# Attention scores: each head in its own 32 partitions of the stacked queries and keys, plain and turned scores issued alternately, other PSUM banks

## The chip, the cores and the metric

The kernel runs on one core of a Trainium2 chip. The metric is the device time of one execution in microseconds (us); lower is better. TensorE multiplies, VectorE (DVE) and ScalarE (ACT) and GpSimd (POOL) work on elements, SyncE (SP) issues the DMAs. PE in a row of the profile is a matmul of TensorE and PEld a load of its stationary operand.

## The reference, cut to what matters

Four residual layers act on `x`, 64 batches of 64 channels by 256 positions. The change touches only the first, a gated cross attention with 8 heads of 8 channels:

```python
x = x + jnp.tanh(g_xattn[0]) * _L0_xattn_ref(_layernorm(x, axis=-1), ctx_2048, ...)
# in _L0_xattn_ref(x, c, ...): b=64, h=8 heads, kc=8 channels of a head, 256 positions
q = _rope(_proj(Wq, bq, x) per head, 4);  k = _rope(_proj(Wk, bk, c) per head, 4);  v = _proj(Wv, bv, c) per head
scores = jnp.einsum('bhqd,bhkd->bhqk', q, k) / jnp.sqrt(kc)
out = jnp.einsum('bhqk,bhkd->bhqd', jax.nn.softmax(scores, axis=-1), v)
return _proj(Wo, bo, out)
```

A mixture of experts, a gated pooling and a feed-forward layer follow. They are the same code in both kernels.

## The kernel before, in words

The attention works on 32 tiles `n` of two batches each (128 channels on the partitions, 256 positions along them), so 16 heads (`HP`) a tile. It is a pipeline over tiles written out by hand: each engine runs the same `body(n, c, i)` for n from -2 to 33, of which the first four and the last four are unrolled and the others run in a loop of four (`steps`). Each body has 16 slots, `s_` 0 to 15, and in body n an engine does its share of the projections of tile n+2, of the plain scores of tile n+1 and of the turned scores of tile n, in the order that the slots give.

A score is computed twice. The plain score (line 510) has queries on the partitions and keys along them: DVE takes its maximum along each row (`tensor_reduce`, line 369) and nothing else is done with it. The turned score (line 527) has keys on the partitions; the row maxima are subtracted in the product itself, by extra rows of the stacked operands, and ACT takes its exponential into `e_t` (line 422). Then `e_t` is multiplied with the values (line 546, "PV" below), 8 products for each group of four heads, each into its own 32 columns of the array and its own 32 partitions of `o_ps`.

Queries and keys are split into a high and a low fp32r part, and three products of parts make one score. These lie as stacked rows: `q_st` holds 96 rows (three times 32: four heads of a unit by 8 channels) and 8 rows for the maxima (`m_rows`); `k_st` has a copy for each of the four heads `j` of a unit, with zeros in the rows of the other three heads. So every score product runs over 96 or 104 rows of the array. A DMA of 32 KB puts each piece of a key there, 12 for a tile (line 211), three of 128 KB the queries (line 225).

PSUM has 8 banks of 2 KB a partition. `s_ps` has two buffers of two banks (a pair of heads each), `st_ps` two of one bank, `o_ps` and `misc` one each. `misc` is used in turn by everything else that TensorE makes: the projections of keys and queries (line 433), the values (471), the turned maxima (461), the turned outputs (488, 494) and the output projection (441). The plain scores of pair g wait for `max_taken` of pair g-2; the turned ones of a head wait for the exponential two heads back.

DVE also makes the statistics of the layer norm (305, 310), normalizes (331), applies the rotation with the bias (295), adds the bias of the values (342) and normalizes the outputs (352, 356). POOL adds the two terms of the rotation (260), splits the sum into high and low (268, 270), makes the reciprocal deviation (247, 249) and adds the result to x (254).

## Time and profile before

| | us |
|---|---|
| median of 3 runs (lowest to highest) | 1603.46 (1603.43 to 1603.86) |
| the profiled execution's own time | 1603.07 |
| its span, first to last instruction | 1601.4 |
| attention, until its last addition to x ends | 588.6 |
| PE busy over the span | 1450.3 |
| DVE, ACT, POOL busy over the span | 957.3, 779.5, 525.7 |

The page divides the span into 40 slices. The attention is the first 14 of them and most of the next. TensorE is busy for 90% or more of the third to the fourteenth slice, and the granted clock is at nine tenths or more of full speed in each of these 14. Matmuls are pipelined, so a busy TensorE says that one is under way, not that the array is full: times between starts tell more than durations. In a timeline, one row stands for consecutive instructions of one line, "x4" says how many, and square brackets hold the idle time of the engine before them and what ended it.

### The profile page before, as it was taken

Reading aid. Unit: us, or ns where it says so; the run is one execution under the profiler, and the core shown is the slowest. Engines: PE = TensorE matmul, PEld = TensorE weight load, DVE = VectorE, ACT = ScalarE, POOL = GpSimd, SP = SyncE. Lnnn points to the kernel's source line nnn. Section 1 sums busy time; section 2 is a strip of 40 time slices with the busy share of each in tenths; the row PEclk is TensorE's granted clock in tenths of the full one; section 3 lists DMA queues with packets and bytes.
Section 4 is the critical chain, followed back from the end, with each engine's and each line's share of the span. In section 5 each row is a group of like instructions: output and inputs, shape, how many; then the busy total and the mean of one; then the engine's idle time right before and its main releaser. Section 6 shows DMA issues by size and latency. Waiting matters only on the chain. (4 is left out here: it accounts for less than half of the span.)

```text
span 1601.4 us, 32051 instructions
## 1 busy us (share of the span) xinstructions
PE 1450.3 (91%) x10096; PEld 1207.3 (75%) x10097; DVE 957.3 (60%) x1819; ACT 779.5 (49%) x1427; POOL 525.7 (33%) x586
## 2 busy tenths in 40 slices
PE   4899999999999958999898999999916599999998
PEld 3677777777777737888787888888805478888887
DVE  6888887878888726766664333333323366666643
ACT  3466666666666653332233333333313366666652
POOL 4332332323323113644356333200041355555220
PEclk9999999999999987999999999999955599999999
DMA  5122122121121112211373323211170001111000
GB/s 170 57 58 63 50 62 55 52 61 53 53 62 52 45 33 67 92 54 53 122 235 109 92 92 92 66 52 52 44 244 0 27 27 40 40 41 40 15 14 27
DMA packets 89017, 106.54 MB, mean 67 GB/s; under 512 B 12144, under 2 KB 80368, under 8 KB 88304
## 3 DMA queue, kind: packets, MB, share of 16 engines
q1 hardware_dynamic: 79488, 75.69, 15.8%
q0 software_dynamic: 9456, 29.89, 5.8%
q8 instruction: 43, 0.70, 0.2%
q14 instruction: 30, 0.25, 0.0%
HBM read 54.29 MB, written 25.03 MB: 50 GB/s over the span
## 5 line engine op out<-in xcount | busy, mean ns | idle before, releaser
L422 ACT ACTIVATE e_t<-st_ps 128x512 f32<-128x512 f32 x512 | 277.9, 595 | 165.4 <-PE st_ps L527 164.9
L369 DVE TENSOR_REDUCE row_max<-s_ps 128x4 f32<-128x1024 f32 x256 | 311.0, 1217 | 34.0 <-PE s_ps L510 33.8
L510 PE MATMUL s_ps<-k_st,q_st 96*128 96x256 f32 x1024 | 197.2, 316 | 14.3 <-DMA q_st<-q_part 13.0
L527 PE MATMUL st_ps<-q_st,k_st 104*128 104x256 f32 x1024 | 170.4, 287 | 1.6 <-ACT e_t L422 1.5
L510 PEld LDWEIGHTS s_ps<-k_st,q_st 96*128 96x128 f32 x1024 | 147.9, 194 | 23.2 <-DMA q_st<-q_part 13.7
L527 PEld LDWEIGHTS st_ps<-q_st,k_st 104*128 104x128 f32 x1024 | 143.9, 190 | 6.6 <-ACT e_t L422 5.2
L546 PE MATMUL o_ps<-e_t,v_st 128*32 128x256 f32 x2048 | 137.1, 385 | 0.9 <-ACT e_t L422 0.9
L1576 POOL DMA_INDIRECT gathered_tail<-sorted_results,result_at x64 | 72.9, 1139 | 153.5 <-POOLq L2046 135.2
L1434 PE MATMUL y_ps_moe<-w_all_moe,h_hi_moe 128*128 x568 | 112.5, 281 | 2.6 <-DVE h_lo_moe L1253 2.6
L1810 DVE TENSOR_TENSOR h_all_tail<-silu_tail,u_ps_tail 128x512 f32<-128x512 f32 x64 | 43.8, 685 | 117.4 <-ACT silu_tail L1684 65.9
L1259 DVE TENSOR_TENSOR h_all_moe<-silu_moe,u_ps_moe 128x512 f32<-128x512 f32 x71 | 48.8, 687 | 106.2 <-PE u_ps_moe L1412 106.2
L1412 PE MATMUL g_ps_moe<-w_all_moe,xt_hi_moe 128*128 x284 | 106.2, 415 | 0.0
L949 ACT COPY y_sb_moe<-y_ps_moe 128x256 f32<-128x256 f32 x71 | 26.5, 373 | 159.3 <-PE y_ps_moe L1434 159.3
L1412 PE MATMUL u_ps_moe<-w_all_moe,xt_hi_moe 128*128 x284 | 99.8, 392 | 0.0
L1434 PEld LDWEIGHTS y_ps_moe<-w_all_moe,h_hi_moe 128*128 128x128 f32 x568 | 92.4, 190 | 6.2 <-issue 3.5
L1249 DVE TENSOR_TENSOR xt_lo_moe<-t_ps_moe,xt_hi_moe 128x256 fp32r<-128x256 f32 x71 | 30.1, 424 | 92.2 <-ACT xt_hi_moe L936 92.2
L818 POOL DMA_INDIRECT sorted_rows<-xn_moe,slots_moe x64 | 64.2, 1004 | 63.1 <-DVE slots_moe L1052 45.8
L546 PEld LDWEIGHTS o_ps<-e_t,v_st 128*32 128x32 f32 x2048 | 53.4, 109 | 40.2 <-ACT e_t L422 1.1
L247 POOL TENSOR_SCALAR var_eps<-mean_var 128x1 f32<-128x1 f32 x32 | 7.5, 235 | 229.8 <-DVE mean_var L310 228.7
L1434 PE MATMUL y_ps_moe<-w_all_moe,h_lo_moe 128*128 x284 | 79.7, 281 | 0.0
L1684 ACT ACTIVATE silu_tail<-g_ps_tail 128x512 f32<-128x512 f32 x64 | 38.0, 594 | 83.9 <-PE g_ps_tail L1964 83.7
L1976 PE MATMUL y_ps_tail<-w_hi_tail,h_hi_tail 128*128 128x256 f32 x256 | 74.1, 289 | 0.5 <-DVE h_lo_tail L1817 0.5
(309 smaller groups left out, 3583.2 us busy)
## 6 DMA issues: line engine op xcount, KB each, us to landing
k_st<-k_part SPq DMA_DIRECT2D x384, 32.0 KB
q_st<-q_part SPq DMA_DIRECT2D x96, 128.0 KB, 3.2
stage_moe<-in_experts POOLq DMA_DIRECT2D x21, 512.0 KB, 4.2
rows_in_moe<-sorted_rows SPq DMA_DIRECT2D x71, 128.0 KB, 2.0
sorted_results<-y_sb_moe SPq DMA_DIRECT2D x71, 128.0 KB
c_in<-in_ctx SPq DMA_DIRECT2D x33, 128.0 KB, 2.1
xn_moe<-in_ctx SPq DMA_DIRECT2D x8, 512.0 KB
context_tail<-in_ctx SPq DMA_DIRECT2D x4, 1024.0 KB, 15.3
```

The costliest lines, as they stand in the source:

```text
L369: nc.vector.tensor_reduce(out, s_ps[s_ // 2 % 2][:].rearrange("p (j h) t -> p j h t", j=2), AX_X, ALU.max).then_inc(s["max_taken"], 1)
L422: nc.scalar.activation(e_t[h % 8][:], st_ps[h % 2][:], ACT.Exp, scale=float(DH) ** -0.5)\
L510: last = nc.tensor.matmul(s_ps[s_ // 2 % 2][:, 2 * (h - s_) + half_, :], q_st[r][0:ROWS, u, half_ * P:(half_ + 1) * P], k_st[r][0:ROWS, u, ...
L527: last = nc.tensor.matmul(st_ps[h % 2][:, half_, :], k_st[r][0:MROWS, u, j, half_ * P:(half_ + 1) * P], q_st[r][0:MROWS, u, :], start=True ...
L546: last = nc.tensor.matmul(o_ps[32 * j:32 * j + 32, u % 2, :], v_st[r][:, half_, u * UH + j, :], e_t[(u * UH + j) % 8][:, half_, :], start= ...
L818: pool.indirect_dma_start(out=xs[:, :], out_offset=bass.IndirectOffsetOnAxis(ap=slots[:, w, GT * j + t:GT * j + t + 1], axis=0), in_=xn[j ...
L1259: nc.vector.tensor_tensor(h_all[c % 2][:], silu[c % 2][:], u_ps[c % 2][:], ALU.mult)\
L1412: last = nc.tensor.matmul(bank[c % 2][:], t[b][:, kc * P:(kc + 1) * P], w_flat[:, bass.ds(where + ((w * 3 + kc) * PIECE + base), FF)], sta ...
L1434: last = nc.tensor.matmul(y_ps[:, 2 * ((c - 1) % 2), :], h[:, m * P:(m + 1) * P], w_flat[:, bass.ds(where + ((w * 3 + 2) * PIECE + m * D), ...
L1576: pool.indirect_dma_start(out=gathered[r][:], out_offset=None, in_=ys[:, :], in_offset=bass.IndirectOffsetOnAxis(ap=result_at[:, q // GT, ...
L1810: nc.vector.tensor_tensor(h_all[m % 2][:], silu[m % 2][:], u_ps[n % 2][:], ALU.mult)\
L1976: last = nc.tensor.matmul(y_ps[:, t, :], h[:, m, t * P:(t + 1) * P], w[:, 2, m * D:(m + 1) * D], start=(m == 0 and b == 0 and t % 2 == 0), ...
```

## The change

The stacked rows are laid out anew. Head j of a unit has partitions 32j to 32j+31 of `q_st` and of `k_st`: three rows for each channel (the three products of parts) and, in every fourth row, the two rows of the maxima (`MAX_ROWS`, 8 rows in all). A score product takes its operands from these 32 partitions alone, so it runs in 32 rows of the array. `k_st` has no copies for four heads any more; 3 DMAs of 128 KB fill it. The rows of the maxima are set to zero in `q_st` by another DMA (`zero_rows`) before the plain scores, and the maxima are written there before the turned ones.

TensorE issues the two products of a turned score and the two of a plain one alternately, one head of each in a slot; they lie in different 32 partitions. The turned scores run 10 slots behind (`LAG`) instead of 8. `s_ps` is now one tensor of three banks; pair p takes two of them in turn (`pair_banks`), and its second head waits for the maxima of the pair just before. `misc` becomes `misc_a` and `misc_b`.

Work moves: the normalization of x from DVE to POOL, in two steps; the bias of the rotation is made once (`turned_bias`) and added on POOL for each tile, so that DVE's rotation is one multiplication of 512 columns; the values are copied by ACT, and their bias goes into `out_bias` once. A pair in banks 0 and 2 needs two reductions on DVE. In the first bodies other buffers are cleared, and eight bodies at the end are unrolled instead of four.

In a body of the changed kernel, TensorE has other work ahead of the scores in slots 1 (turn `a_sb`), 2 (turn the maxima), 3 (project k), 5 (output projection), 6 (project q), 8 (turn `o_sb`), 10 (values) and 14 (turn `o_sb`); PV follows the scores of slots 3, 7, 11 and 15. POOL makes the parts of k, the addition to x, the parts of q and then the normalization of tile n+3. The diff below holds, in this order, the constants, the buffers, SP's stacking, POOL's sum with the bias, DVE's order and its reductions, ACT's copy of the values, and TensorE's scores.

```diff
-    LAG = 8
-    ROWS, MROWS = 96, 104
-    PEEL_FIRST, PEEL_LAST = (-2, -1, 0, 1), (30, 31, 32, 33)
+    PAIRS = HP // 2
+    LAG = 10
+    MAX_ROWS = slice(3, P, 16)
+    PEEL_FIRST, PEEL_LAST = (-2, -1, 0, 1), tuple(range(26, 34))
...
-        s_ps = [ps(f"s_ps{r}", [P, 4, D]) for r in range(2)]
+        s_ps = ps("s_ps", [P, 3, 2, D])
...
+        pair_banks = [((0, 1), (0, 2), (1, 2))[p % 3] for p in range(PAIRS)]
+        pair_order = [(1, 0) if p == 0 or p % 3 == 1 else (0, 1) for p in range(PAIRS)]
...
                     sp.wait_ge(s["k_high"], n + 3)
+                    for t in range(2):
+                        sp.dma_start(k_st[r][t:P:4, :, :].bitcast(F32), part["k"][:, 0, :].bitcast(F32))\
+                            .then_inc(k_stacked[r], 16)
                     sp.wait_ge(s["k_split"], n + 3)
+                    sp.dma_start(k_st[r][2:P:4, :, :].bitcast(F32), part["k"][:, 1, :].bitcast(F32))\
+                        .then_inc(k_stacked[r], 16)
+                    sp.wait_ge(s["q_high"], n + 3)
+                    for t in (0, 2):
+                        sp.dma_start(q_st[r][t:P:4, :, :].bitcast(F32), part["q"][:, 0, :].bitcast(F32))\
+                            .then_inc(q_stacked[r], 16)
...
+                nc.gpsimd.tensor_tensor(bare[a][:], roped[a][:, 0, :], roped[a][:, 1, :], ALU.add)\
+                    .then_inc(s[a + "_summed"], 1)
+                pool.wait_ge(s[a + "_summed"], n + 3)
+                nc.gpsimd.tensor_tensor(whole[a][:], bare[a][:], turned_bias[a][:], ALU.add).then_inc(s[a + "_whole"], 1)
...
+                for p in range(PAIRS):
+                    if p == 0 and there(n, c, 0):
+                        split_max(n, c)
+                    if there(n, c, 1):
+                        take_max(n, c, p)
+                    if p == 1 and there(n, c, 2):
+                        rope_parts("k", n, c)
+                    if p == 3 and there(n, c, 2):
+                        rope_parts("q", n, c)
+                    if p == 4 and there(n, c, -1):
+                        normalize_out(n, 0)
+                    if p == 5 and there(n, c, 3):
+                        stats_of(n, 3)
+                    if p == 7 and there(n, c, -1):
+                        normalize_out(n, 1)
...
+                if high == low + 1:
+                    last = nc.vector.tensor_reduce(out, s_ps[:, low:high + 1, :, :], AX_X, ALU.max)
+                else:
+                    for at, bank in enumerate((low, high)):
+                        last = nc.vector.tensor_reduce(out[:, at, :], s_ps[:, bank, :, :], AX_X, ALU.max)
...
+                        nc.scalar.copy(v_st[r][:, :, :, 0:DH],
+                                       misc_a[:, 0:2 * P].rearrange("p (a h d) -> p a h d", a=2, d=DH))\
+                            .then_inc(s["v_stored"], 1)
...
+                rows = slice(32 * j, 32 * j + 32)
+                return [(s_ps[:, pair_banks[p][at], half_, :], q_st[r][rows, u, half_ * P:(half_ + 1) * P],
+                         k_st[r][rows, u, :]) for half_ in range(2)]
...
+                        wait_count(pe, s["exp_done"], HP * (n + k) + h - 1)
+                        wait_alone(pe)
...
+                        wait_count(pe, s["max_taken"], (n + 1) * PAIRS + s_ // 2 - (s_ + 1) % 2)
+                    for half_ in range(2):
+                        if turned:
+                            out, w, of = turned[half_]
+                            last = nc.tensor.matmul(out, w, of, start=True, stop=True)
+                            if half_ == 1:
+                                last.then_inc(s["st_scored"], 1)
+                        if scores:
+                            out, w, of = scores[half_]
+                            last = nc.tensor.matmul(out, w, of, start=True, stop=True)
+                            if half_ == 1 and s_ % 2 == 1:
+                                last.then_inc(s["scored"], 1)
```

## Rows read from the trace of the kernel before

**Rows 1.** Busy time by stretch: us, PE, PEld, DVE, ACT, POOL, granted clock, DMA share, GB/s.
```profile
300.00:400.00 100.00, 99.21 (x901) 78.71 (x902) 80.80 (x138) 63.38 (x124) 30.34 (x53) 1.00 0.21 57
...
590.00:600.00 10.00, 0.95 (x5) 0.96 (x6) 4.96 (x21) 3.12 (x5) 2.22 (x6) 0.50 0.38 127
```
**Rows 2.** Timeline of TensorE, the turned maxima of bodies 1 and 29.
```profile
61.03 0.27 PE L461 MATMUL misc<-ident,m_parts 128*64 128x128 f32 x1
...
534.24 0.27 PE L461 MATMUL misc<-ident,m_parts 128*64 128x128 f32 x1
```
**Rows 3.** Waits, 100 to 500 us: us in total, times, longest us.
```profile
ACT e_t L422 <- PE st_ps L527: 123.0, 165, 1.9
```
**Rows 4.** Groups of instructions, 100 to 500 us: busy us, mean ns of one, idle before.
```profile
L369 DVE TENSOR_REDUCE row_max<-s_ps 128x4 f32<-128x1024 f32 x190 | 231.2, 1217 | 21.7 <-PE s_ps L510 21.5 <-issue 0.2
...
L510 PE MATMUL s_ps<-k_st,q_st 96*128 96x256 f32 x760 | 144.8, 313 | 0.0
...
L546 PE MATMUL o_ps<-e_t,v_st 128*32 128x256 f32 x1520 | 101.7, 385 | 0.0
...
L342 DVE TENSOR_TENSOR v_st<-misc,bias_v 128x128 f32<-128x128 f32 x48 | 11.5, 281 | 0.0
```
**Rows 5.** Timeline of TensorE over one body: start us, us from first start to last end.
```profile
249.98 0.82 PE L510 MATMUL s_ps<-k_st,q_st 96*128 96x256 f32 x4
...
252.90 1.07 PE L546 MATMUL o_ps<-e_t,v_st 128*32 128x256 f32 x16
253.90 0.66 PE L488 MATMUL misc<-ident,o_sb 128*128 128x128 f32 x4
254.31 0.72 PE L510 MATMUL s_ps<-k_st,q_st 96*128 96x256 f32 x4
254.87 0.64 PE L527 MATMUL st_ps<-q_st,k_st 104*128 104x256 f32 x4
255.35 0.61 PE L488 MATMUL misc<-ident,o_sb 128*128 128x128 f32 x4
...
258.08 0.72 PE L510 MATMUL s_ps<-k_st,q_st 96*128 96x256 f32 x4
...
261.65 1.13 PE L433 MATMUL misc<-c_in,w_in 128*128 128x256 f32 x4
262.43 0.82 PE L510 MATMUL s_ps<-k_st,q_st 96*128 96x256 f32 x4
...
266.88 0.83 PE L510 MATMUL s_ps<-k_st,q_st 96*128 96x256 f32 x4
```
**Rows 6.** Timeline of DVE in the same body.
```profile
254.59 0.26 DVE L352 RECIPROCAL o_rcp<-misc 128x16 f32<-128x16 f32 x1 [0.69 <-PE misc L488]
...
255.09 1.22 DVE L369 TENSOR_REDUCE row_max<-s_ps 128x4 f32<-128x1024 f32 x1
...
258.84 1.23 DVE L369 TENSOR_REDUCE row_max<-s_ps 128x4 f32<-128x1024 f32 x1 [0.91 <-PE s_ps L510]
259.98 0.42 DVE L305 BATCH_NORM_STATS2 stats<-x_sb 128x6 f32 x1
...
260.71 0.18 DVE L316 TENSOR_SCALAR m_parts<-row_max 128x32 fp32r<-128x32 f32 x1
...
261.10 1.23 DVE L369 TENSOR_REDUCE row_max<-s_ps 128x4 f32<-128x1024 f32 x1
```
**Rows 7.** Timeline of the first bodies, where a plain score waits for a maximum.
```profile
35.99 4.62 DVE L369 TENSOR_REDUCE row_max<-s_ps 128x4 f32<-128x1024 f32 x4
...
37.27 0.74 PE L510 MATMUL s_ps<-k_st,q_st 96*128 96x256 f32 x4 [0.84 <-DVE row_max L369]
```
**Rows 8.** Timeline of POOL in the same body as rows 5.
```profile
251.32 0.73 POOL L260 TENSOR_TENSOR q_whole<-q_roped 128x256 f32<-128x256 f32 x1 [2.35 <-DVE q_roped L295]
...
252.69 0.73 POOL L270 TENSOR_TENSOR q_part<-q_whole,q_part 128x256 fp32r<-128x256 f32 x1
```
**Rows 9.** DMA issues of the page: KB each, median us from issue to landing.
```profile
q_st<-q_part SPq DMA_DIRECT2D x96, 128.0 KB, 3.2
```

More of the change, by code:

```diff
@@ L273, in _ @@
+                    row = x_row(n - 2)
+                    nc.gpsimd.tensor_tensor(row, row, like_row(n, y_sb), ALU.add).then_inc(s["y_free"], 1)
+                if there(n, c, 2):
+                    parts_of("q", n, c, i)
+                if there(n, c, 3):
+                    normalize(n, 3)
             steps(pool, body)
@@ L286, in _, with rope_parts @@
+            dve.wait_ge(s["bias_summed"], 2)
             clear_values((0,))
[L287 to L291 removed]
+            def rope_parts(a, n, c):
                 dve.wait_ge(s[a + "_projected"], n + 3)
                 wait_count(dve, s[a + "_summed"], n + 2)
[L294 to L298 removed]
@@ new lines, in take_max @@
+            def take_max(n, c, p):
+                g = (n + 1) * PAIRS + p
+                dve.wait_ge(s["scored"], g + 1)
+                if p == 0:
+                    wait_count(dve, s["m_split"], n)
+                u, j = 2 * p // UH, 2 * p % UH
+                out = row_max[(c + 1) % 2][:].rearrange("p (j u h) -> p j u h", j=UH, u=UNITS)[:, j:j + 2, u, :]
+                low, high = pair_banks[p]
+                if high == low + 1:
[3 more added lines that the diff above has]
+                        last = nc.vector.tensor_reduce(out[:, at, :], s_ps[:, bank, :, :], AX_X, ALU.max)
+                last.then_inc(s["max_taken"], 1)
@@ L437, in body, with score_turned @@
+            def score_turned(c, k, h):
+                r, u, j = (c + k) % RING, h // UH, h % UH
+                rows = slice(32 * j, 32 * j + 32)
+                return [(st_ps[h % 2][:, half_, :], k_st[r][rows, u, half_ * P:(half_ + 1) * P], q_st[r][rows, u, :])
+                        for half_ in range(2)]
             def body(n, c, i):
                 for s_ in range(HP):
-                    if s_ == 0 and there(n, c, -2):
-                        pe.wait_ge(s["a_taken"], n - 1)
-                        nc.tensor.matmul(misc[:, 0:D], w_out[:], a_t[:], start=True, stop=True)\
-                            .then_inc(s["y_projected"], 1)
@@ L445, in body @@
+                    if s_ == 3 and there(n, c, 2):
                         if isinstance(n, int) and n < 2:
@@ L530, in body @@
-                        last.then_inc(s["st_scored"], 1)
+                                pe.wait_ge(ones_in, 16 * RING)
+                        wait_count(pe, s["exp_done"], HP * (n + k) + h - 1)
+                        wait_alone(pe)
+                    if there(n, c, 1):
+                        scores = score(n, c, s_)
+                        if s_ == 0:
+                            pe.wait_ge(q_stacked[(c + 1) % RING], 64 * uses(c, i, 1))
+                            pe.wait_ge(k_stacked[(c + 1) % RING], 48 * uses(c, i, 1))
+                            if isinstance(n, int) and n == -1:
+                                pe.wait_ge(ones_in, 16 * RING)
+                        wait_count(pe, s["max_taken"], (n + 1) * PAIRS + s_ // 2 - (s_ + 1) % 2)
@@ L550, in body, with turn_out, value_bias @@
                         last.then_inc(s["pv_done"], 1)
-            steps(pe, body)
+            def turn_out(b):
+                for half_, u in ((h, u) for h in range(2) for u in range(2)):
+                    at = (2 * half_ + u) * P
+                    last = nc.tensor.transpose(misc_b[:, at:at + P], o_sb[b][:, u, half_ * P:(half_ + 1) * P],
+                                               ident[:])
+                last.then_inc(s["o_turned"], 1)
+            def value_bias():
+                pe.wait_ge(more_consts_in, 3 * 16)
+                nc.tensor.matmul(misc_b[:, 0:1], w_out[:], bias[:, 5:6], start=True, stop=True)\
+                    .then_inc(s["value_bias_made"], 1)
+            steps(pe, body, None, value_bias)
 def experts(nc, dram, x, ident, tanh_gain, xs, ys, result_at, shares, attn, half_rotated):
```

419 lines of the change are left out of this document (183 added, 236 removed).

## The prediction

> **What bounds the kernel now.** I read the busy time by stretch first, to find the stage. In the attention TensorE is busy 99.2 of 100 us, DVE 80.8, ACT 63.4, POOL 30.3, at the full clock [rows 1]. The maxima of bodies 1 and 29 are turned 473.2 us apart, 28 bodies of 16.90 us each [rows 2]; these 28 are what the change can move. Then the waits: ACT waits for turned scores 123 us in 400, TensorE for nobody to speak of [rows 3]. So a body lasts as long as TensorE's instructions take, and the starts in its timeline say which. Between the first and the last of rows 5 lie 31 rows, one body. A group of four score products in mid-stream takes 0.48 us, 0.12 each (254.87 to 255.35), up to 0.66 where another kind of work has come before it; the 16 groups make 9.5 us. The four PVs take 1.00 each, start to next start [rows 5], 4.0 in all. The rest (projections, turns) adds to 3.35. Sum 16.9.
>
> PV shows what the change is after. One of its products lasts 385 ns on average, yet 16 are through in 1.00 us [rows 4, 5], because four neighbours use different columns and run together. The scores, 313 ns each on average [rows 4], run one behind the other.
>
> **TensorE after the change.** The same 64 score products, each over 32 rows, in 16 slots of two turned and two plain. No row of before shows products in different rows of the array at once. Bounds for a slot: nothing overlaps, 4 x 0.12 = 0.48; the two kinds overlap fully, 0.24. I take 0.24, nearest to PV's rows, where four overlap. 16 x 0.24 = 3.84, in place of 9.5. The Trainium skill (TensorE: Matmul & The Clock Gate, Part 3, "Measured speedup vs the span model") gives 3.07 times for four such row groups, 77% of the full factor; 77% of two would make a slot 0.31. No run here has shown it yet; by it the sum would be 16 x 0.07 = 1.1 us a body dearer on TensorE, part of it before pairs that DVE waits for.
>
> What it adds on TensorE: changes between products of 32 rows and full ones. The price is read at PV, which is of another shape than its neighbours: four passes of a full fp32 product take 0.78 (261.65 to 262.43), so four rounds of PV should take 0.78 and take 1.00 [rows 5]; 0.22 for entering and leaving, 0.11 a change. Eight groups of other work now stand between scores, one of them right behind a PV: 15 new changes, 1.65 us. They cost nothing at the least (turns and scores now follow each other without loss, 0.41 + 0.56 for eight products [rows 5]), and I put the upper bound at 0.3 each, nearly the whole of a product in flight. The skill speaks against the change here (TensorEngine Tiling (Array Packing), Key Properties): changing the tiling mode drains TensorE. It has no price; by rows it is the 0.11. TensorE: 3.84 + 4.0 + 3.35 + 1.65 = 12.8 us a body, 4.1 under now.
>
> **DVE after.** Its starts price it: a reduction of 1024 holds it for 1.14 (258.84 to 259.98); statistics 0.73 (to 260.71), split of the maxima 0.39 (to 261.10), normalizing half the outputs 0.50 (254.59 to 255.09) [rows 6]. From 281 ns for 128 columns and 1217 for 1024 [rows 4] a column costs 1.045 ns; so 512 columns take 0.68, or 0.59 in a row of them, and the new rotation 0.6. Five reductions of 1024 and three pairs of 512: 5 x 1.14 + 3 x 1.18 = 9.2; rotations 1.2, outputs 1.0, statistics 0.73, split 0.39: 12.5 us. Now it is 13.7 (80.8% of 16.90). Gone are the normalization of x and the bias of the values.
>
> **The wait that is added.** This decides the size. Before, a pair of plain scores needed the maxima of two pairs back, and DVE was never in the way. With three banks, the second head of pair p (slot 2p+1) waits for the maxima of pair p-1, and since that wait stands ahead of the slot's turned products too, everything on TensorE queues behind it. DVE in turn cannot begin pair p until that slot is done. The round trip: from DVE's end to TensorE's start 0.06 (first of four reductions ends at 37.21, product at 37.27 [rows 7]); first to last product of the slot 0.13, and 0.08 that a first product takes longer; from the last product's start to DVE 0.32 (group at 258.08, last product 0.44 later, reduction at 258.84 [rows 5, 6]). With the 0.08 by which a reduction's end lies behind its hold, DVE stands idle for 0.67 to 0.69 between two maxima unless it has something else to do. Its other work covers that after pair 5 (statistics) and between tiles (outputs and split), and nearly after pairs 1 and 4; after pairs 2 and 6, and after pair 0, there is none.
>
> Walked through a body, zero where the last maxima of the tile before are known, pairs at TensorE's slots: pair 0 is scored at 0.5, DVE comes at 0.8 (outputs, split), done 1.9. Pair 1: TensorE waits for the split, turns, projects k, scored 2.8; DVE idle 0.8. Two reductions, rotation, 4.5. Pair 2 follows PV and the output projection, 4.7, idle 0.2, done 5.8. Pair 3 waits for it behind the projection of q: 6.5, idle 0.7; maxima and rotation to 8.3. Pair 4 after PV and turn: 8.5, idle 0.2; to 10.2 with the outputs. Pair 5: 10.3, idle 0.2; to 12.2 with statistics. Pair 6 in time; to 13.3. Pair 7: 14.0, idle 0.7; to 15.2, known 15.3. So 12.5 of work and 2.8 of idle time: 15.3 us.
>
> **POOL and the queue.** One more sum of 0.73 for k and for q each, and two or so for x [rows 8]: 5.1 to 8.1 us, hidden by itself. But the chain to the next tile's plain scores gets longer. q is rotated at 8.3; POOL is just through with k and x, and needs 2.1 (251.32 to 253.42 [rows 8]) and 0.89 for the extra sum: 11.5. The last of three DMAs leaves SP at about 11.9 and lands 3.2 later [rows 9], at 15.1. Slot 0 would start at 14.7 (15.3 less the 0.57 to its pair's end). It comes 0.4 late; DVE, busy until 16.1 with outputs and split, and the 0.8 of idle time at pair 1 absorb nearly all. I add 0.1: 15.4 us. The 9 DMAs a body instead of 17 don't shorten it.
>
> ACT gets one copy (about 0.3) to its 10.7: 11.0, hidden while it is the third engine. If it weren't, that would be 0.3 a body.
>
> **Sum.** 28 bodies x 1.5 = 42 us. At the start TensorE waits for the queue chain, which grows by the extra sums: 2 us dearer over bodies -1 and 0; what is cleared there differs little. At the end the bodies without projections gain about 1 each, two more slots of lag cost one: -3 in all. 1603.1 (the profiled execution, 0.4 under the median) - 42 + 2 - 3 = 1560. The other layers stay. With 15.0 to 16.0 a body the forecast's own range is 1543 to 1577.
>
> **The rivals.** *The hand-over hardly binds* (0.16): DVE meets its scores in time except at the three places where nothing covers the trip, 12.5 + 3 x 0.69 = 14.6, saves 2.3 a body, 1538. For it: TensorE has 2.6 us to spare. Against: that slack isn't where the waits are.
>
> *Changes between shapes are dear* (0.16): at 0.3 each they add 15 x 0.19 = 2.9 on TensorE, of which about 1 falls before pairs that DVE waits for: 16.4, 28 x 0.5 = 14 saved, 1588. A quarter of this case ends within 0.2% of now.
>
> *Rows don't overlap* (0.13), the change doesn't do what it says: a slot takes 0.48, pairs are scored 0.23 later behind each wait, and TensorE, 16.6 us busy, comes late at pairs 2, 4 and 5. The same walk gives 17.6, and 28 x 0.7 = 20 more: 1623. This is the rival on the other side: the new wait is paid and nothing is had for it. A slot of 0.38 is about where it turns. Against it stands PV in the trace.
>
> *The clock falls* (0.05), as it does where TensorE is idle between stages, 0.50 [rows 1]. What products over a quarter of the rows do to the clock, no row shows. TensorE's 12.8 at half speed is nearly 24 us with waits: 1800. Nothing in the trace points to it; PV, with few columns a product, runs at 1.00.
>
> **How the numbers follow.** The forecast has 0.50. The range takes in the hand-over rival and the dear changes, 1534 to 1605, and leaves out the last two, 0.18. Faster by over 0.2% (below 1600.3, about what a measurement of this kernel tells from no change): 0.50 + 0.16 + 0.12 = 0.78. Within: 0.04 + 0.01 of the third = 0.05. Slower: 0.12 + 0.05 = 0.17.
>
> **What would show it.** Right: turned maxima 15.4 us apart; plain and turned products starting within 0.02 us of each other; four of a slot in about 0.24; DVE's largest wait is for plain scores, 0.5 to 0.8 us at pairs 1, 3 and 7, and TensorE's for `row_max`; its DMA wait small. Wrong: no such waits on DVE (first rival), gaps on PEld of over 0.3 us at each change (second), products 0.12 apart (third), a clock of 0.5. The prediction fails most easily if TensorE's work lies otherwise between the pairs than I walked it, since idle times of 0.2 stand beside others of 0.8, or if the queue is slower with rows four partitions apart, which no row of before shows.

## The result, and the profile after

The changed kernel takes 1678.26 us, median of 4 runs (1676.05 to 1679.46), against 1603.45 for the kernel before on the same chip: a ratio of 1.0465, 95% interval 1.0452 to 1.0479. It was forecast to be faster, at 1560 us with a range up to 1605; sign and range are both wrong. The profiled execution's span is 1677.8 us, 76.4 longer.

Where these 76.4 us are is read from the turned maxima of bodies 1 and 29, as in [rows 2]. Timeline of TensorE after; the middle two stand around one body at the full clock:

```profile
62.34 0.42 PE L501 MATMUL misc_b<-ident,m_parts 128*64 128x128 f32 x1
...
360.29 0.30 PE L501 MATMUL misc_b<-ident,m_parts 128*64 128x128 f32 x1
...
377.68 0.30 PE L501 MATMUL misc_b<-ident,m_parts 128*64 128x128 f32 x1
...
580.26 0.30 PE L501 MATMUL misc_b<-ident,m_parts 128*64 128x128 f32 x1
```

The 28 bodies last 517.9 us, 18.50 each in place of 16.90: 44.7 of the 76.4. A body in which the clock does not fall takes 17.39, as here (377.68 - 360.29), to 17.5, most often 17.45. From the maxima of body 29 to the end of the attention 82.5 us pass in place of 54.4: another 28.2. The start costs 1.3 and the other layers 2.2. The busy time by stretch, columns as in [rows 1]: the 28 bodies, the tail behind them, the moments before and after one fall of the clock, and 400 us in the middle:

```profile
62.34:580.26 517.92, 469.45 (x4287) 272.41 (x4283) 360.98 (x588) 307.72 (x615) 219.56 (x363) 0.93 0.17 53
580.26:662.80 82.54, 68.19 (x479) 36.86 (x477) 25.76 (x44) 40.39 (x79) 8.81 (x13) 0.66 0.04 12
...
387.80:391.20 3.40, 2.51 (x32) 1.31 (x28) 3.10 (x7) 2.44 (x7) 1.91 (x4) 1.00 0.23 77
391.30:394.60 3.30, 3.30 (x28) 1.77 (x28) 1.88 (x4) 1.49 (x3) 1.46 (x4) 0.50 0.29 88
100.00:500.00 400.00, 363.60 (x3321) 210.87 (x3319) 279.26 (x453) 238.33 (x478) 171.10 (x282) 0.92 0.17 53
```

TensorE, busy 99.2% before, is busy 90.9%, and its granted clock, 1.00 before, is 0.92 to 0.93 in the loop and 0.66 in the tail. It falls to 0.50, the 1.2 GHz level, for about 75 us of the loop in 18 spells of a few us and for 56 us of the tail. The first of the 28 bodies belongs to this too: the clock is on record only from 70.4 us on, but up to there TensorE's rows last as long as at the low level (0.42 for the turn at 62.34, 0.30 for the same turn later), and this body takes 19.69. So three things happened: the body at the full clock got 0.55 longer (28 x 0.55 = 15 us), the low clock in the loop cost 28 x 18.50 - 28 x 17.45 = 29, of it 2 in the first body, and in the tail up to 28. The 28 are an estimate: 56 us at half clock do the work of 28 where TensorE is the limit, and 54.5 would be left, the tail of before. But TensorE idles for 14 of the 82.5 us, so it may be less.

The waits, 100 to 500 us (us in total, times, longest), against [rows 3]:

```profile
ACT e_t L454 <- PE st_ps L561: 162.2, 197, 2.1
...
DVE row_max L368 <- PE s_ps L566: 59.9, 65, 2.1
PEld st_ps L561 <- issue: 57.2, 166, 0.7
DVE row_max L365 <- PE s_ps L566: 52.1, 66, 2.6
...
PEld misc_b L592 <- ACT o_sb L432: 19.9, 21, 0.9
PEld st_ps L561 <- DVE row_max L368: 19.5, 36, 0.8
```

DVE waits 112 us for plain scores in 400/18.5 = 21.6 bodies, 5.2 a body, and TensorE waits for DVE's maxima and for a copy of ACT. Each waits for the other. No DMA is among the large waits. Next, TensorE's timeline in the body behind the 17.39 us one. It starts at 377.68, runs at the full clock up to a fall at 391.2, and takes 18.36:

```profile
378.77 1.13 PE L465 MATMUL misc_a<-c_in,w_in 128*128 128x256 f32 x4 [0.37 <-ACT a_t L422]
...
381.26 0.38 PE L561 MATMUL st_ps<-q_st,k_st 32*128 32x256 f32 x1
381.26 0.38 PE L566 MATMUL s_ps<-k_st,q_st 32*128 32x256 f32 x1
381.48 0.28 PE L561 MATMUL st_ps<-q_st,k_st 32*128 32x256 f32 x1
381.49 0.28 PE L566 MATMUL s_ps<-k_st,q_st 32*128 32x256 f32 x1
381.69 0.70 PE L514 MATMUL misc_b<-a_t,w_out 128*128 128x256 f32 x2
...
388.16 0.38 PE L561 MATMUL st_ps<-q_st,k_st 32*128 32x256 f32 x1 [0.20 <-DVE row_max L368]
...
391.25 1.12 PE L592 MATMUL misc_b<-ident,o_sb 128*128 128x128 f32 x4 [0.75 <-ACT o_sb L432]
```

Turned and plain products start within 10 ns of each other, as was hoped. But the second product of the same 32 rows starts 0.22 after the first, not 0.12 as in [rows 5], and the next work 0.43 after the slot's start. Two at a time, at half the rate each: 0.11 a product, the old pace. The weight loads (PEld) of the same four products:

```profile
381.26 0.18 PEld L561 LDWEIGHTS st_ps<-q_st,k_st 32*128 32x128 f32 x1 [0.41 <-issue]
381.26 0.18 PEld L566 LDWEIGHTS s_ps<-k_st,q_st 32*128 32x128 f32 x1
381.37 0.18 PEld L561 LDWEIGHTS st_ps<-q_st,k_st 32*128 32x128 f32 x1
381.37 0.18 PEld L566 LDWEIGHTS s_ps<-k_st,q_st 32*128 32x128 f32 x1
```

The load for the second half starts 0.11 after the first product did, and the second product another 0.11 later. This is no matter of the 32 rows. In the kernel before, the first step of a group of scores behind other work is 0.20 to 0.22 as well (254.31 to 254.51), and the last one before a PV 0.21 (before a turn, 0.12); the steps between them are 0.12, each load starting together with the running product. The same steps stand in the last bodies of changed_filled_wait (below), where six turned products of the same 32 rows follow each other at the full clock:

```profile
604.82 0.74 PE L563 MATMUL st_ps<-q_st,k_st 32*128 32x256 f32 x4
605.40 0.40 PE L567 MATMUL st_ps<-q_st,k_st 32*128 32x256 f32 x2
605.73 0.30 PE L501 MATMUL misc_b<-ident,m_parts 128*64 128x128 f32 x1
```

Their steps are 0.23, four times 0.12, and 0.21 to the turn. So a slot by itself has no step of 0.12 at all: it is one first step and one last step, 0.43, with two groups of rows or with four.

DVE in the same body, against [rows 6]:

```profile
377.81 1.23 DVE L365 TENSOR_REDUCE row_max<-s_ps 128x4 f32<-128x1024 f32 x1 [0.28 <-PE s_ps L566]
380.39 1.29 DVE L368 TENSOR_REDUCE row_max<-s_ps 128x2 f32<-128x512 f32 x2 [1.35 <-PE s_ps L566]
...
382.89 1.22 DVE L365 TENSOR_REDUCE row_max<-s_ps 128x4 f32<-128x1024 f32 x1 [0.61 <-PE s_ps L566]
384.74 1.23 DVE L365 TENSOR_REDUCE row_max<-s_ps 128x4 f32<-128x1024 f32 x1 [0.62 <-PE s_ps L566]
...
386.81 1.29 DVE L368 TENSOR_REDUCE row_max<-s_ps 128x2 f32<-128x512 f32 x2 [0.25 <-PE s_ps L566]
...
393.22 1.29 DVE L368 TENSOR_REDUCE row_max<-s_ps 128x2 f32<-128x512 f32 x2 [1.43 <-PE s_ps L566]
```

Idle for 0.28 + 1.35 + 0.61 + 0.62 + 0.25 + 1.43 = 4.5 us before six of its eight pairs, where 2.8 was forecast. The two large ones follow TensorE's waits for ACT at 378.77 and 391.25; part of the last is the fall of the clock at 391.2.

A slot does not always take 0.43. When the next slot follows without a wait, its products lie in the other two groups of 32 rows and start before the slot is through, so that both share a first and a last step: two slots then pass in 0.44 to 0.79. TensorE's time in bodies without a fall, added up from start to start of its kinds of work, with its idle time apart (mean us a body, of 11 bodies after the change and 22 or 23 elsewhere; two columns are runs of the next section):

| | before | forecast | tiled_two_banks_each | two_banks_with_handover | after |
|---|---|---|---|---|---|
| scores, 16 slots | 9.4 | 3.84 | 4.8 | 5.65 | 6.3 |
| PV | 4.0 | 4.0 | 4.0 | 4.0 | 4.0 |
| other work, with the changes between shapes | 3.35 | 5.0 | 5.3 | 5.2 | 5.2 |
| idle | 0.1 | 2.6 | 1.8 | 2.1 | 1.9 |
| body | 16.9 | 15.4 | 15.9 | 16.96 | 17.45 |

So a slot takes 0.40 on average after the change, and 0.30 where two banks a pair let the slots follow each other.

### The profile page after: what moved, and what is told of

Read it like the earlier page. It is cut to its first block and busy times, and to the rows that moved or that the text cites. A ratio compares the mean times of both kernels' runs of the same rounds, so it can differ in the third digit from the quotient of the medians.

```text
span 1677.8 us, 32160 instructions
## 1 busy us (share of the span) xinstructions
PE 1472.3 (88%) x10098; PEld 1111.3 (66%) x10099; DVE 931.2 (55%) x1763; ACT 773.8 (46%) x1455; POOL 606.8 (36%) x716
## 5 line engine op out<-in xcount | busy, mean ns | idle before, releaser
L454 ACT ACTIVATE e_t<-st_ps 128x512 f32<-128x512 f32 x512 | 300.0, 600 | 261.9 <-PE st_ps L561 261.1
L365 DVE TENSOR_REDUCE row_max<-s_ps 128x4 f32<-128x1024 f32 x160 | 195.9, 1225 | 90.2 <-PE s_ps L566 86.2
L561 PE MATMUL st_ps<-q_st,k_st 32*128 32x256 f32 x1024 | 230.0, 353 | 16.8 <-DVE row_max L368 6.2
L566 PE MATMUL s_ps<-k_st,q_st 32*128 32x256 f32 x1024 | 228.3, 355 | 16.2 <-DMA q_st<-q_part 6.9
L561 PEld LDWEIGHTS st_ps<-q_st,k_st 32*128 32x128 f32 x1024 | 143.1, 203 | 141.9 <-issue 92.9
L368 DVE TENSOR_REDUCE row_max<-s_ps 128x2 f32<-128x512 f32 x192 | 123.7, 686 | 91.8 <-PE s_ps L566 91.8
L583 PE MATMUL o_ps<-e_t,v_st 128*32 128x256 f32 x2048 | 163.0, 444 | 1.2 <-ACT e_t L454 1.2
L566 PEld LDWEIGHTS s_ps<-k_st,q_st 32*128 32x128 f32 x1024 | 141.0, 203 | 21.4 <-DVE row_max L365 8.4
L273 POOL TENSOR_TENSOR k_bare<-k_roped 128x256 f32<-128x256 f32 x32 | 23.3, 727 | 231.7 <-DVE k_roped L343 231.7
L583 PEld LDWEIGHTS o_ps<-e_t,v_st 128*32 128x32 f32 x2048 | 59.0, 121 | 52.1 <-issue 20.9
```

The costliest lines, as they stand in the source:

```text
L365: last = nc.vector.tensor_reduce(out, s_ps[:, low:high + 1, :, :], AX_X, ALU.max)
L368: last = nc.vector.tensor_reduce(out[:, at, :], s_ps[:, bank, :, :], AX_X, ALU.max)
L454: nc.scalar.activation(e_t[h % 8][:], st_ps[h % 2][:], ACT.Exp, scale=float(DH) ** -0.5)\
L561: last = nc.tensor.matmul(out, w, of, start=True, stop=True)
L566: last = nc.tensor.matmul(out, w, of, start=True, stop=True)
L583: last = nc.tensor.matmul(o_ps[32 * j:32 * j + 32, u % 2, :], v_st[r][:, half_, u * UH + j, :], e_t[(u * UH + j) % 8][:, half_, :], start= ...
```

## The experiments

The theory: a slot of 0.43 by itself means that the new rows gain little on TensorE, the three-bank hand-over costs more than that, and the clock takes the rest. The rivals: the new rows themselves are slow, alternation is needed, the waits for ACT or the moved work are the cost. Each ratio is against the kernel before on the same chip. A run without an interval was timed once, beside medians of the kernel before of 1604 to 1611; "full clock" is the usual body without a fall, and "low" the recorded us at half clock in the loop and in the tail.

**tiled_two_banks_each** is the kernel before with the new rows and the alternate issue alone: `LAG` 8, two buffers of two banks, and DVE's, POOL's and ACT's work as before.

```diff
-    ROWS, MROWS = 96, 104
+    MAX_ROWS = slice(3, P, 16)
...
-        k_st = [sb(f"k_st{r}", [P, UNITS, UH, D], F32R) for r in range(RING)]
+        k_st = [sb(f"k_st{r}", [P, UNITS, D], F32R) for r in range(RING)]
...
+                r, h = (c + 1) % RING, s_ ^ 2
+                u, j = h // UH, h % UH
+                rows = slice(32 * j, 32 * j + 32)
+                return [(s_ps[s_ // 2 % 2][:, 2 * (h % 2) + half_, :], q_st[r][rows, u, half_ * P:(half_ + 1) * P],
+                         k_st[r][rows, u, :]) for half_ in range(2)]
```

> The kernel before with the 32-partition layout alone: one turned and one plain head issued alternately in a slot, but two buffers of two banks for the plain scores, one misc bank, and DVE's, ACT's and POOL's work as before (the plain heads of a unit in another order, so that the two heads of a slot lie in different partitions). Theory 1, pace of the products: two products side by side cost 0.22 us and not 0.12, and a change between shapes some 0.28, so TensorE has 6.9 + 4.0 + 3.35 + 8 x 0.28 = 16.5 us a body and the kernel comes out near 1595, within 15. Theory 2, the hand-over over three banks made the change slow: it is gone here, TensorE's 12.8 us lie under DVE's 13.7, 1510 to 1530. Theory 3, the clock falls because of products over 32 rows: bodies differ by 2 to 4 us among each other as in the changed kernel, 1610 to 1650.

Measured: 1587.84 us (1583.94 to 1590.79), ratio 0.9894 (0.9861 to 0.9928). Most bodies take 15.88 us, and the clock stays at 1.00 in the loop; in the tail it is 0.73:

```profile
100.00:500.00 400.00, 354.43 (x3851) 211.72 (x3843) 345.94 (x579) 270.73 (x529) 130.93 (x227) 1.00 0.20 63
511.60:574.70 63.10, 53.88 (x443) 29.56 (x443) 24.18 (x40) 36.31 (x71) 6.51 (x10) 0.73 0.05 15
```

So the new rows are worth 1.02 us a body, no more, and they alone bring the kernel 1% under the old time: the loop gains 24 us in all, and the tail, with its clock, gives 9 back. That is in the range of the first theory, but not by its sum: the scores take less (4.8) and TensorE stands idle for 1.8 us a body. Two slots that follow each other pass in 0.72 here, not 0.86, and most of the idle time stands before products into the one `misc` bank:

```profile
301.11 0.37 PE L527 MATMUL st_ps<-q_st,k_st 32*128 32x256 f32 x1 [0.25 <-issue]
...
301.40 0.35 PE L527 MATMUL st_ps<-q_st,k_st 32*128 32x256 f32 x1
...
301.83 1.07 PE L549 MATMUL o_ps<-e_t,v_st 128*32 128x256 f32 x16
...
PE misc L468 <- DVE k_roped L295: 15.5, 25, 0.6
...
PE misc L478 <- DVE q_roped L295: 13.7, 26, 0.5
```

**tiled_four_groups** is that kernel with the eight products of two turned and two plain heads together in every second slot, so that all four groups of rows have work at once. The two turned heads then also wait for the exponentials of the two before them together.

```diff
-                    if s_ % 1 == 0:
+                    if s_ % 2 == 0:
                         k, h = st_head(s_)
-                        heads = range(1)
+                        heads = range(2)
```

> As the run before, but in every second slot two turned and two plain heads are issued together: first halves of all four, then second halves, in four different groups of 32 rows. Theory 1: eight products take about 0.44 us instead of 0.88, as in the few places of the changed kernel where two slots met; TensorE 3.5 + 4.0 + 3.35 + 2.2 = 13.1 us a body, under DVE's 13.7 with some waits, 14.3: 1520 to 1540. Theory 2 (hand-over only): the same as the run before, since that is bound by DVE already. Theory 3 (clock): some bodies 2 us and more longer, 1560 to 1600.

Measured: 1601.44 us (1597.99 to 1609.56), ratio 0.9987 (0.9969 to 1.0006): no gain, and outside all three ranges. TensorE's timeline and stretch, then the wait that shows why:

```profile
301.09 0.38 PE L527 MATMUL st_ps<-q_st,k_st 32*128 32x256 f32 x1 [0.38 <-DVE row_max L370]
...
301.32 0.28 PE L532 MATMUL s_ps<-k_st,q_st 32*128 32x256 f32 x1
301.53 0.85 PE L549 MATMUL o_ps<-e_t,v_st 128*32 128x256 f32 x12
...
100.00:500.00 400.00, 321.98 (x3737) 181.04 (x3738) 337.25 (x562) 260.09 (x511) 126.15 (x218) 1.00 0.19 61
...
PEld st_ps L527 <- DVE row_max L370: 57.3, 110, 1.3
```

Eight products pass in 0.44, 0.055 each, no longer than the four of a slot: the factor of two that I had put into a slot is had only by putting more products between the same first and last step. TensorE's busy time falls to 80%, and it waits for DVE instead; the body is 16.4, and the clock stays at 1.00 in the loop.

**two_banks_with_handover** is tiled_two_banks_each, in which the second head of a pair also waits for the maxima just before, as three banks force it to.

```diff
-                            wait_count(pe, s["max_taken"], (n + 1) * (HP // 2) + s_ // 2 - 1)
+                            wait_count(pe, s["max_taken"], (n + 1) * (HP // 2) + s_ // 2 - (s_ + 1) % 2)
```

> The run with the new rows and two banks for each pair of plain scores (body 15.88 us), with one edit: the second head of a pair waits for the maxima of the pair just before, as three banks force it in the changed kernel. The wait isn't needed here; it is put in to read its price alone. If the hand-over between TensorE and DVE is the larger part of the changed kernel's loss: 1 to 1.6 us a body more, 16.9 to 17.5, 1615 to 1635. If that loss comes from the order of work around misc, the two reductions of a split pair and the waits for ACT: under 0.4 us a body, 1586 to 1600. The clock theory (it falls where only products over 32 rows and idle time come together) expects some dips again if bodies get longer.

Measured: 1626.33 us, ratio 1.0128 (1.0106 to 1.0150). The body goes from 15.88 to 16.96 with nothing else touched. The wait alone costs 1.08 us a body, which uses up the gain of 1.02. By the table, 0.84 of it is time in the scores, because neighbouring slots no longer run into each other, and 0.27 is idle time. The rest of the 1.3% lies outside the usual body: 6 us before the loop, 5 in it (mostly its first body and a fall of the clock; low 10), and 10 in the tail.

**changed_half_max** is the changed kernel with the row maximum taken over half of the keys, which halves DVE's share of the round trip.

```diff
-                    last = nc.vector.tensor_reduce(out, s_ps[:, low:high + 1, :, :], AX_X, ALU.max)
+                    last = nc.vector.tensor_reduce(out, s_ps[:, low:high + 1, :, 0:P], AX_X, ALU.max)
```

> The changed kernel, but the row maximum is taken over half of the keys (128 of 256 columns of each head's row), so a reduction holds DVE about half as long; a shift of the exponent cancels in the softmax. DVE's work falls from 12.5 to about 8.4 us a body and each round trip of a bank by 0.5 us. If the hand-over over three banks is what makes the body 17.4 us at full clock: 3 to 4 us a body less, 1560 to 1590. If TensorE's own pace and its waits for ACT do: at most 1 us a body less, 1645 to 1675. The clock theory expects dips as before or more of them, since TensorE has no more to do.

Measured: 1616.4 us, between the two ranges. Full clock 16.65, 0.8 less (22 us); that is what was expected if TensorE's own pace and its waits for ACT set the body, not the 3 to 4 of the hand-over. Low is 10 and 28 in place of 75 and 56. Of the 62 us, 23 more are the low clock in the loop, 13 the tail and 4 the start.

**changed_old_rows** is the changed kernel with the old rows of 96 and 104, and 15 DMAs to stack them; banks, order, `LAG` and moved work stay changed.

```diff
-    MAX_ROWS = slice(3, P, 16)
+    ROWS, MROWS = 96, 104
...
+                    for j in range(2, UH):
+                        for t, of in enumerate((0, 0, 1)):
+                            stack_k(j, t, of)
```

> The changed kernel with the layout alone put back: scores over 96 and 104 rows, 12 pieces of k and one q stack as before; three banks, order, LAG 10 and the work moved to POOL and ACT stay. If the three banks and the order of work are what costs (the two-bank run with the new rows was faster than before), this is no faster than the changed kernel: a slot takes 0.48 instead of 0.43 us and the changes between shapes fall away, 17 to 18 us a body, 1610 to 1670. If the clock falls because of the products over 32 rows, the dips are gone here and all bodies last the same, near 17.4. If it falls because of the idle times of this order, the dips stay.

Measured: 1718.11 us, ratio 1.0671 (1.0638 to 1.0705): worse than the change, outside what I expected of either theory. The body at the full clock is 19.6; low is 11 and 0 in place of 75 and 56, though TensorE is no busier (358.5 of 400 us) and idles 2.1 us a body. The new rows save 2.1 of it. The rest of the change costs 2.7 a body with the old rows (1.9 of it idle time of TensorE), part of it a DMA wait that the new rows do not have:

```profile
PEld st_ps L558 <- DMA k_st<-k_part: 22.2, 21, 1.3
```

**changed_not_alternated** issues the two turned products first, then the two plain ones.

```diff
-                    for half_ in range(2):
-                        if turned:
...
+                    for half_, (out, w, of) in enumerate(turned):
+                        last = nc.tensor.matmul(out, w, of, start=True, stop=True)
...
+                    for half_, (out, w, of) in enumerate(scores):
+                        last = nc.tensor.matmul(out, w, of, start=True, stop=True)
```

> The changed kernel with the two products of the turned score first and then the two of the plain one, instead of alternately. Theory 1: the products of one 32-row group wait for each other's weights (0.22 apart), so only the second turned and the first plain one overlap: about 0.66 instead of 0.43 a slot, up to 3.5 us a body where nothing else waits; 1710 to 1760. If the alternation is worth nothing, because the array takes weights for one product at a time: within 1% of 1678.

Measured: 1681.49 us, as the change. Full clock 17.4 to 17.6, low 68 and 62. A first plain product still starts before the second turned one, which stands ahead of it in the program:

```profile
396.82 0.38 PE L559 MATMUL st_ps<-q_st,k_st 32*128 32x256 f32 x1
396.82 0.38 PE L563 MATMUL s_ps<-k_st,q_st 32*128 32x256 f32 x1
397.04 0.27 PE L559 MATMUL st_ps<-q_st,k_st 32*128 32x256 f32 x1
397.05 0.27 PE L563 MATMUL s_ps<-k_st,q_st 32*128 32x256 f32 x1
```

**changed_copy_earlier** takes the second copy of `o_ps` on ACT a slot earlier, for the wait at 391.25.

```diff
-                    if s_ in (5, 13) and there(n, c, -1):
-                        b = s_ // 13
+                    if s_ in (5, 12) and there(n, c, -1):
+                        b = s_ // 12
```

> The changed kernel with one edit on ACT: the second copy of o_ps stands one slot earlier (12 instead of 13). TensorE's wait in slot 14 for this copy (0.75 to 1.0 us a body, and DVE's 1.4 us before pair 7) shrinks by the 0.5 us of the exponential that goes ahead of it now. If that wait is on the path: 0.4 to 0.6 us a body less, 1655 to 1667, and fewer dips of the clock if the dips come from idle time. If only the bank hand-over binds: within 3 us of 1678.

Measured: 1666.33 us. At the full clock only 0.08 a body is gained: TensorE idles 0.4 less, and its scores take 0.3 more. Low in the loop is 34 in place of 75. The time is in the expected range for the wrong reason.

**new_rows_lighter_dve** adds to tiled_two_banks_each the changed kernel's moves: normalization of x on POOL, copy of the values on ACT, their bias folded.

```diff
-                        nc.vector.tensor_scalar(out, row, mean_var[:, 0:1], rstd[:], ALU.subtract, ALU.mult)\
-                            .then_inc(s["xn_ready"], 1)
...
+                        nc.scalar.copy(v_st[r][:, :, :, 0:DH],
+                                       misc[:, 0:2 * P].rearrange("p (a h d) -> p a h d", a=2, d=DH))\
+                            .then_inc(s["v_stored"], 1)
```

> The run with the new rows and two banks for each pair (1588), and DVE relieved in two places as the changed kernel does it: the normalization of x on POOL, the values copied by ACT with their bias folded in once. DVE's work falls from 13.7 to 12.9 us a body. That run's body of 15.88 us has TensorE 14.1 busy and waits on misc and on DVE's maxima. If DVE's order is what holds misc: 0.4 to 0.8 us a body less, 1565 to 1577. If misc itself does (one bank, each user waits for the one before): under 0.2, 1583 to 1590.

Measured: 1591.31 us, ratio 0.9891 (0.9866 to 0.9915), body 15.88 again. DVE is relieved (330.5 of 400 us busy in place of 345.9) and nothing comes of it, as expected if the one `misc` bank holds TensorE up; the time is 1 us over that range.

**changed_filled_wait** asks whether idle time makes the clock fall: two full products ahead of the wait at 391.25, their result overwritten, and in the bodies without plain scores each turned product three times.

```diff
                         pe.wait_ge(s["o_normed"], 2 * (n - 1) + 1)
+                        for _ in range(2):
+                            nc.tensor.matmul(misc_b[:, 0:D], w_out[:], rope[:, 0, :], start=True, stop=True)
...
+                    if turned and not scores:
+                        for _ in range(2):
+                            for out, w, of in turned:
+                                nc.tensor.matmul(out, w, of, start=True, stop=True)
```

> The changed kernel with work for TensorE in its waits: two full products of 256 columns (0.8 us, results overwritten) ahead of the wait for the copy in slot 14, and in the last bodies, where there are no plain scores, each turned product made three times (same result). If the clock falls because TensorE stands idle there: the dips become rare, bodies 17.5 to 17.7, and the last bodies run at full clock: 1625 to 1650, faster with more work. If idle time has nothing to do with it: dips as before and some 0.2 us a body more, 1680 to 1700.

Measured: 1683.7 us. In the loop low falls to 24 and the mean body to 17.87, and no fall begins at the filled wait any more. In the tail nothing is gained, though TensorE is now busy nearly all the time:

```profile
600.00:655.00 55.00, 53.31 (x327) 36.89 (x327) 3.86 (x13) 20.26 (x38) 1.45 (x2) 0.59 0.01 2
```

**changed_taller_fill** keeps the fill of the loop, and in the last four bodies passes the first half of each PV, over 128 rows, two times more instead.

```diff
-                        for half_ in range(2):
+                        again = 2 if isinstance(n, int) and n >= 30 else 0
+                        for half_, stop in ((0, True),) * again + ((0, False), (1, True)):
```

> The changed kernel with the filled wait in slot 14 as before (two full products), and in the last four bodies, instead of tripled turned products, two more passes of the first half of each PV (128 rows of the array, overwritten by the real one, same result; 1.0 us more for each PV). If the clock falls in the last bodies because products over 32 rows count for less, the work over all rows holds it at full: the stretch from the turned maxima of body 29 to the end of the attention takes 65 to 75 us instead of 82.5 (97.5 with tripled turned products), 1650 to 1668 in all. If any work is as good as another or none helps: 90 us and more, 1675 to 1690.

Measured: 1665.45 us. Low in the tail is 10 in place of 68; the tail itself, 77.2, is a little over what was expected:

```profile
572.50:649.70 77.20, 66.82 (x671) 38.16 (x669) 25.74 (x44) 39.93 (x79) 8.81 (x13) 0.93 0.04 13
```

The mean body is 18.21 with the very loop of the run above (17.87): the falls in a loop scatter by that much.

**changed_short_fill** is the control: the same fill in the loop, over 32 rows, and nothing added in the last bodies.

```diff
-                            nc.tensor.matmul(misc_b[:, 0:D], w_out[:], rope[:, 0, :], start=True, stop=True)
+                            nc.tensor.matmul(misc_b[:, 0:D], w_out[0:32, :], rope[0:32, 0, :], start=True, stop=True)
```

> The control for the filled wait: the same two products of 256 columns ahead of the wait in slot 14 of the changed kernel, but over 32 rows of the array instead of 128 (results overwritten); nothing is done in the last bodies. From the turned maxima of body 1 to those of body 29 the changed kernel had 75 us at the lower clock and 18.50 us a body, with products over all rows 24 and 41 us (two runs) and 17.87 and 18.21. If products over 32 rows count for less: 60 us and more at the lower clock, 18.3 to 18.7 a body, 1673 to 1688. If any product in the wait does as well: 20 to 45 us, 17.8 to 18.2, 1657 to 1668.

Measured: 1661.97 us, ratio 1.0348 (1.0272 to 1.0423), low 24 in the loop, none of it beginning at the filled wait, and 47 in the tail. As a filling of that wait, products over 32 rows help as much as full ones, so my theory that rows are what the clock counts fails there.

**two_banks_taller_fill** puts the same repeats of PV into tiled_two_banks_each.

> The best run so far (new rows, two banks for each pair, 1588) with the same two more passes of the first half of each PV in the last four bodies. There its clock was 0.5 for the last 23 us of the attention, and the stretch from the turned maxima of body 29 took 63.2 us, against 54.3 in the kernel before. If work over all rows holds the clock: 56 to 60 us, 3 to 7 us less in all, 1581 to 1585. If not: 4 to 16 us more, 1592 to 1604.

Measured: 1586.58 us, ratio 0.9892 (0.9865 to 0.9918), between the two ranges. The tail's clock is 0.95 in place of 0.73 and the tail 64.9 us in place of 63.1: the extra products cost what the clock gives back.

Of these, tiled_two_banks_each is the version that beats both kernels. The two others at 0.989 can't be told from it and have more in them.

## Why the prediction was wrong

**The step that failed** is the slot: "I take 0.24, nearest to PV's rows, where four overlap". A slot by itself takes 0.43, and the average slot of the change 0.40; the term 16 x 0.24 = 3.84 measured 6.3. The 0.24 is two steps at the pace of a long run, 0.12. That pace holds within 32 rows too (changed_filled_wait), but a slot has two products of each group and so only a first step of 0.22, behind other work, and a last one of 0.21, before other work. The rows of before had both: groups of four took up to 0.66 behind another kind of work, against 0.48 in mid-stream. I had bounds of 0.24 and 0.48, and took the wrong end. The second half of the step is that the added wait parts neighbouring slots, which would otherwise fill all four groups; the prediction had no term for that. In two_banks_with_handover the scores take 5.65 a body, without the wait 4.8. The Trainium skill's figure (TensorE: Matmul & The Clock Gate, Part 3, "Measured speedup vs the span model") is for four row groups; scaling it to two gave me an estimate of 0.31. This case's traces do not agree with it: a slot by itself takes 0.43, and four groups are 2.2 times as fast as the old pace (eight products in 0.44 against four in 0.48). tiled_two_banks_each comes to 0.30 a slot, but because its slots run into each other over four groups. What two groups reach in a long run, no run here shows.

With 0.43 in the same sum, TensorE would need 16 x 0.43 = 6.9, + 4.0 + 3.35 + 1.65 = 15.9 a body, and tiled_two_banks_each measured 15.88. That they agree is chance: its scores take 4.8 and its idle time is 1.8. The changes between shapes make other work 5.2 to 5.3 us in place of 3.35, 1.85 to 1.9 where 1.65 was forecast; what was left out is their share in the scores. Against the forecast body of 15.4, the 17.45 of the change have 2.5 more in the scores, 0.2 more in the changes and 0.7 less idle time.

**Two rivals share the cause.** On TensorE it is the second, "Changes between shapes are dear", at 0.16: above 3.84 + 4.0 + 3.35 the change needs 4.4 us a body, 0.29 for each of the 15 changes counted, where that rival had 0.3. But it let only 1 us of its 2.9 reach the body (16.4). By the time it is the third, "Rows don't overlap", at 0.13. The rows do overlap, but its slot of 0.48 is near the 0.40 to 0.43 measured. Its walk gave 17.6 and named 0.38 as the point where it turns (16.9); between them 0.40 to 0.43 give 17.0 to 17.25. The body is 17.45. The hand-over's waits were thus placed rightly: `row_max` waits on TensorE, scores late on DVE. The isolated wait costs 1.08 a body. 15.88 + 1.08 = 16.96, and some 0.5 remain. It lies with the rest: TensorE's two waits for ACT, which the walk did not have, the other order and the pairs in two reductions. I did not separate these; moving one copy brought 0.08.

**DVE's work** was right: 12.5 forecast, 360.98 busy us in 28 bodies are 12.9. Its idle time, 2.8 forecast, is 4.5 to 5.2. POOL and the queue are hidden, as said: no DMA wait.

**The clock** had 0.05. "Nothing in the trace points to it" was true of the trace of before, where TensorE hardly waited in the loop (0.1 us a body). It costs 29 us in the loop and up to 28 in the tail, 57 of 76. In the loop, the 18 falls begin at two places: nine right behind TensorE's wait of some 0.75 us for ACT's copy, as at 391.25, and nine some 1.6 us into a body, behind a wait of about half a us for DVE and one of 0.28 for ACT (at 412.7 and 414.5 before the fall at 415.1). In the three runs that fill the first wait no fall begins there (5 or 6 are left, all at the second place), and with half the maximum the three that are left all begin there. The time at half clock shrinks from 75 to 10 to 41 us where waits are shortened or filled. So the first of these waits brings falls on; the second was not filled in any run. But waits alone do not: two_banks_with_handover idles as much (2.1 us a body) and has low 10, and the old rows with the change's banks, order and waits have 11. Four groups at 80% busy and two banks at 89% have no recorded fall in the loop at all, so busy time alone does not tell either. In the tail, 32-row products kept TensorE 97% busy at 0.59, repeats of PV brought 0.93, and the old rows have 1.00. What exactly is counted stays open: the old rows had few falls in the loop and none in the tail, as if the rows mattered, while as a filling of the wait 32 rows did as well as 128.

**The sum.** The start (+2 forecast, +1.3) was right. The end was forecast at -3 and measured +28.2; by the estimate above it would be as before without the falls, so the 3 us of gain did not come either. From 1560 to the 1679.5 of the profiled execution, 28 x 2.05 = 57 us are the body at the full clock, 29 the low clock in the loop, 31 the tail, and under 2 the start and the other layers together. The lower end of the forecast's own range does not follow from its sum: 15.0 us a body gives 1603.1 - 53.2 + 2 - 3 = 1549, not 1543.

## What to carry to other kernels

When products are made small to run side by side, do not price a short group by the pace of a long run: here a group cost its first and its last step, 0.43 us, whether four or eight products stood in it, in two or four groups of rows. Put more products between two changes of shape, and ask which added wait keeps them apart. Before PSUM is divided anew, count the buffers between producer and consumer: one bank less made each hand-over a round trip, and its 1.08 us a body was more than the 1.02 that the rows gained. When a change takes TensorE from busy to waiting, its clock becomes a term of the sum, here the largest. And when a sum meets a measured time, compare its terms too: 15.9 met 15.88 with one term 2 us too large and 1.8 us of idle time left out.

## What was not expected of the hardware

- A group of products of 256 columns that stands between other kinds of work has a first step of 0.20 to 0.23 us and, where the shape changes behind it, a last one of 0.21. Between them the steps are 0.12, over 96 rows as over 32 (before; changed_filled_wait, 604.82 to 605.73). With two products in each group of 32 rows, two groups take 0.43 and four 0.44.
- The hand-over's waits in two_banks_with_handover are short (140 in 400 us, none over 0.5 us). They cost 0.84 us a body by keeping slots in different rows apart, and only 0.27 as idle time.
- Products of different groups of rows need not be issued alternately. Issued turned, turned, plain, plain, they start at 396.82, 397.04, 396.82, 397.05. The Trainium skill (TensorE: Matmul & The Clock Gate, Part 3, The mechanism) says that matmuls start and end strictly in program order; on the starts this trace does not agree.
- TensorE busy for 53.3 of 55 us was granted 0.59 of its clock (changed_filled_wait, 600 to 655 us).
